# The value products of item s-1 move ahead of the first head's probability transposes of item s

## What is computed

```
q, k = rope(heads(h @ wq)), rope(heads(c @ wk));  v = heads(c @ wv)
a = softmax(q @ k^T / 8);  o = a @ v;  x = x + o @ wo + bo
```

## Time and profile before

| | us |
|---|---|
| median of 3 runs | 400.03 (399.65 to 401.43) |
| the profiled execution | 399.18 |
| its span, first to last instruction | 397.4 |
| outside the span (399.18 - 397.4) | 1.8 |
| PE busy | 377.9 (95%) |
| DVE busy | 304.4 (77%) |
| ACT busy | 294.5 (74%) |
| POOL busy | 171.1 (43%) |

### The profile page before, as it was taken

The page is one execution under the profiler, slowest core; times in us unless marked ns, Lnnn a source line. Parts: engine busy times, 40 slices in busy tenths (PEclk is TensorE's granted clock), DMA queues, the critical chain, the costliest instruction groups (busy, mean ns, idle before and its releaser), DMA issues.

```text
span 397.4 us, 9852 instructions
## 1 busy us (share of the span) xinstructions
PE 377.9 (95%) x3597; PEld 284.2 (72%) x3597; DVE 304.4 (77%) x655; ACT 294.5 (74%) x1023; POOL 171.1 (43%) x155
## 2 busy tenths in 40 slices
PE   7989999999999999999999898998999999999987
PEld 3557777776778777777777567775777778788665
DVE  4978998977888777988787758673658978888741
ACT  2377877877868778878787785779679787987932
POOL 4376544445555454554545334340365550302120
PEclk9999999999999999999999999999999999999999
DMA  7133333322333332332211200000000000000001
GB/s 231 54 123 120 107 126 107 120 101 103 125 115 107 106 106 87 129 123 84 81 68 67 82 27 28 2 2 1 2 2 2 2 3 2 2 3 2 2 0 53
DMA packets 17474, 25.90 MB, mean 65 GB/s; under 512 B 3631, under 2 KB 6194, under 8 KB 17426
## 3 DMA queue, kind: packets, MB, share of 16 engines
q1 hardware_dynamic: 17106, 25.05, 18.7%
q10 hardware_dynamic: 288, 0.22, 0.3%
q0 software_dynamic: 32, 0.00, 0.0%
HBM read 8.48 MB, written 0.52 MB: 23 GB/s over the span
## 4 chain that ended last, share of the span: by engine, by line
PE 61%; DVE 18%; ACT 10%; issue 6%; POOL 3%; DMA 1%; SPq 0%; DVEq 0%; POOLq 0%
PE bank L983 49%; PE bank L1069 7%; ACT prob L451 4%; PE bank L1279 4%; DVE nmax L859 3%; DVE xn L671 3%; ACT raw L537 2%; DVE prob L740 2%; DVE nmax L729 2%; DVE qk L771 2%; POOL xn L290 1%; DVE hT L682 1%; DVE qk L761 1%; DVE probT L754 1%; DVE st L656 1%
## 5 line engine op out<-in xcount | busy, mean ns | idle before, releaser
L309 POOL TENSOR_TENSOR swp<-swp,small 128x512 f32<-128x512 f32 x62 | 78.8, 1280 | 53.6 <-PE bank L983 31.7
L451 ACT ACTIVATE prob<-bank,nmax 128x128 f32<-128x128 f32 x256 | 91.5, 391 | 2.2 <-DVE nmax L729 2.2
L537 ACT ACTIVATE raw<-bank,nmax 128x128 f32<-128x128 f32 x256 | 72.9, 390 | 11.6 <-DVE nmax L859 11.3
L729 DVE TENSOR_REDUCE nmax<-bank 128x4 f32<-128x512 f32 x64 | 41.2, 686 | 33.0 <-PE bank L983 33.0
L451 ACT ACTIVATION_READ_ACCUMULATOR prob<-bank,nmax 128x1 f32 x256 | 59.3, 231 | 0.0
L355 POOL TENSOR_TENSOR prob<-prob,rz 128x512 f32<-128x512 f32 x29 | 30.2, 1042 | 58.0 <-DVE rz L734 58.0
L859 DVE TENSOR_REDUCE nmax<-bank 128x4 f32<-128x512 f32 x64 | 41.2, 685 | 17.1 <-PE bank L983 17.1
L983 PE MATMUL bank<-hT,wqkv 128*128 128x512 f32 x96 | 49.1, 595 | 0.2 <-DVE qk L761 0.2
L283 POOL TENSOR_TENSOR rstd<-vare,neg_half 128x4 f32<-128x4 f32 x12 | 12.3, 1024 | 84.1 <-DVE vare L663 84.0
L1069 PEld LDWEIGHTS bank<-small,prob 128*128 128x128 f32 x256 | 28.4, 140 | 24.3 <-DVE prob L740 13.4
L457 ACT ACTIVATE probT<-bank 128x512 f32<-128x512 f32 x32 | 19.1, 597 | 35.1 <-PE bank L1069 35.1
(11 more groups left out here) (114 smaller groups left out, 661.3 us busy)
## 6 DMA issues: line engine op xcount, KB each, us to landing
swp<-raw SPq DMA_DIRECT2D x124, 128.0 KB, 2.1
wqkv<-in_wqkv SPq DMA_DIRECT2D x16, 256.0 KB, 2.8
wff<-in_wff SPq DMA_DIRECT2D x4, 256.0 KB, 3.1
x<-in_x SPq DMA_DIRECT2D x2, 256.0 KB, 4.6
wmod<-in_wmod SPq DMA_DIRECT2D x2, 256.0 KB, 2.7
ctx<-in_ctx SPq DMA_DIRECT2D x1, 384.0 KB, 6.6
ctxT<-in_ctxT SPq DMA_DIRECT2D x1, 384.0 KB, 3.5
wsq<-in_wsq SPq DMA_DIRECT2D x1, 320.0 KB, 2.9
```

Source lines behind the costliest of these rows:

```text
L309: nc.gpsimd.tensor_tensor(four(swp[:, m % 2, f, :]), four(swp[:, m % 2, f, :]), sin[f], ALU.mult).then_inc(rope_sin[f], 1)
L451: last = nc.scalar.activation(prob[:, hh, bcols(u)], S[hh][:, bcols(u)], ACT.Exp, bias=nmax[:, s % 2, hh, u:u + 1], accum_out=zsum[:, s % ...
L537: last = nc.scalar.activation(prob1[:, s % 2, hh, bcols(u)], score_bank(s, hh)[:, bcols(u)], ACT.Exp, bias=nmax[:, s % 2, hh, u:u + 1])
L729: nc.vector.tensor_reduce(nmax[:, s % 2, hh, :], four(S[hh][:, :]), AX.X, ALU.max, negate=True).then_inc(rowmax[hh], 1)
```

## The change

In `l0_slot` of PE, for s = 1 to 29, the eight products `prob_values(s - 1)` are issued ahead of `transpose_probs(s, 0)` rather than behind it. Both keep their own waits. Nothing is added or removed, no transfer moves, and no other engine's list changes.

```diff
                 if s == 31:
                     prob_values(s - 1)
-                transpose_probs(s, 0)
                 if 1 <= s < 30:
                     prob_values(s - 1)
+                transpose_probs(s, 0)
                 if s == 28:
                     pe.wait_ge(exps[0], 29)
                     up(0, 0, 0, S[0])
```

## The result

The changed kernel takes 403.81 us (median of 8 runs) beside 400.11 for the kernel before (8 runs): ratio 1.0102, 95% interval 1.0081 to 1.0123, that is 4.1 us slower (3.2 to 4.9). Beside other runs later it was 1.0089 (1.0064 to 1.0115), 3.6 us. 402.9 had been forecast, 2.9 us slower. Its profiled execution took 404.01, with a span of 402.2.

A forecast was written before the change was run, and what follows sets the result against it. The prediction took PE's instruction list to bound the first layer. Terms 2.1 - 2.2 + 3.0 = +2.9 us took the median from 400.03 to 402.9; range for 8 in 10: 401.0 to 404.4.

The forecast's parts named there:

- What bounds the kernel: First layer is a race along PE's list; weight loads waited 13.4 us for DVE's division, but plain slots lose nothing to it.
- plain slots: Nine first-layer slots without background work or seed row, 6.64 to 6.65 us each, PE busy throughout.
- Part 1, the change of shape: Four array-shape changes per slot instead of three: +0.15 us in each of 14 slots where PE sets the pace, +2.1 us.
- The rival in which it is free: Shape changes cost nothing, covered by the wide fill or the queue: -0.8 us in all, 399.2; chance 0.09.
- The one in which waits at the head of PE's list hold the loads back: Value products' waits delay loads behind them by 0.05 to 0.1 us in 28 slots: 1.4 to 2.8 added, about 405; chance 0.08.
- Part 2, the stalls: Value products fill the transposes' wait for the division in slots 1, 4, 5, 7, 13, 21 and 28: -2.2 us.
- slots 4, 13, 21: Stall of 0.34 us less the 0.15 shape change: 0.19 gained in each, -0.57 us together.
- Slot 28: Transposes start 0.42 us late; number of shape changes stays the same, so the whole 0.42 is gained: -0.42 us.
- Slot 1: No output projection, short PE list; in the new order bound by the rope sum: -0.48 us, length 6.23.
- Slots 5 and 7: Stalls of 0.45 and 0.59 us, each less 0.15 for the shape change: -0.30 and -0.44 us.
- The sentence that no transfer moves and SP follows the slots: Side effects of the swap: no DMA moves, and SP and POOL follow the slots; no term in the sum.
- Part 3, the lost cover: Slots 6, 8, 9, 17, 25, 29: transposes no longer run while value products wait for bank O's readers; +3.0 us.

## Why the prediction was right, and by how much it was off

- **What bounds the kernel**: right. The load waits of 13.4 us were no loss in the plain slots; with them gone these slots are longer.
- **Part 1, the change of shape**: right to 0.01 us a slot (2.56 worked out, 2.57 seen; 0.15 in all 13 plain slots of three kernels). The rival in which it is free is out. The one in which waits at the head of PE's list hold the loads back is out for slots without a late copy; with one, three added waits right ahead of the transposes do cost 0.20, but in an arrangement that the changed kernel doesn't have.
- **Part 2, the stalls**: slots 4, 13, 21 gave 0.20 each (0.19 forecast), and with the old order slots 13 and 21 take 7.43 in every profile, so these stalls belong to the slots. Slot 28 gave 0.52, not 0.42: the wide products, which enter right after another shape, pay an entry of 0.10 that the sum had left out. Slot 1 is the step that failed. The sum gave it -0.48, read from one profile in which its copy was early. Where it is late the rope sum binds either order and the gain is 0; the two profiles of the changed kernel stand 0.45 and 0.75 above the profile that was read. Slots 5 and 7 failed in the same way, though their lengths came out (6.80 and 6.79 for 6.79 forecast). Their whole stalls of 0.45 and 0.59 were late copies: with early ones the old order takes 6.64 in both. In the changed kernel's first profile slot 5 had a copy nearly as late as before, and the order gave 0.13; in the second it was early and the order cost 0.15. In slot 7 the copy was early in both, so the order cost 0.15 there, and the 0.43 of difference is the copy's. That the forecast hit slot 7 is luck as far as the order goes. The sentence that no transfer moves and SP follows the slots missed why: slot 6, longer by 0.58, gives the copy of slot 7 that much more room.
- **Part 3, the lost cover**: 0.58, 0.59, 0.49, 0.40, 0.37 and 0.59 against 0.59, 0.59, 0.50, 0.40, 0.37 and 0.59. Missing was slot 15 in executions with a late copy, where the modulation read of bank O ends late, while the prediction took it to be over in time.
- **The total**: without slots 1 and 15 the sum was 2.9 + 0.48 - 0.15 = +3.2. Over slots 1 to 30, against the profile that was read, the changed kernel has 5.07 - 0.45 - 1.39 = +3.2 in its first profile and 4.13 - 0.75 - 0.15 = +3.2 in its second. That agreement rests on late copies in slots 5, 7 and 19 of the profile that was read. Against the second profile of the kernel before the same sums are 3.75 + 0.32 - 0.59 = +3.5 and 2.81 + 0.03 + 0.65 = +3.5: slot 5 then costs 0.15 instead of giving 0.29, slot 19 costs 0.15 instead of 0.02, and slot 7 gives 0.53. What was off was to take the copies of one execution as given. Had slot 1 been put at 0, the forecast would have been +3.4, 403.4. That lies within the intervals of both measurements, +3.6 (2.6 to 4.6) and +4.1 (3.2 to 4.9); lateness in slot 15 is a candidate for a share of what is left, and it was not separated from chance.

## What to carry to other kernels

A weight load's wait is not a stall: look whether the matmuls behind it still start at full pitch, and move work only in the places where they don't. Before two steps on one engine are swapped, ask of the later one whether it waits for something else: then the earlier one was its cover, and the swap pays it in full. Read a term that hangs on a transfer from several executions, since one may be lucky. And before a stall is booked as a gain, ask whether it belongs to the slot or to a transfer that came late that time: compare executions in which it came at the same moment.

## What the runs showed of the hardware

Switching PE between whole-array, column-tiled (value) and row-tiled (score) products cost 0.09 us on leaving a shape. Entering one cost 0.06 more (two transposes in 0.37 for 0.31) and 0.10 before wide products (the eight of `up` in slot 28: 229.97 - 226.34 = 3.63 in the kernel before, 234.23 - 230.70 = 3.53 in the changed one, where they follow transposes). A wide product ahead didn't hide the exit: 0.95 for 0.86 in slot 11.

The swapped copies, of equal size each time, let the second sine product end anywhere from 4.50 to 6.27 us into slot 1 from one execution to the next. Part of that spread is no transfer: in seven of the twelve profiles this product took 1.27 us and ended at 5.42 or earlier, in five it took 1.72 and ended at 5.98 or later. Between this product and DVE's division either can be the one that waits. In slot 1 of the changed kernel's first profile the division took 1.82 us and POOL's two products 2.51 together; in the second POOL began 0.11 later in the slot, the division took 0.70 and the two products 2.96 (start, duration, what; DVE and POOL of the first, then of the second):

```profile
27.61 1.82 DVE L740 TENSOR_TENSOR prob<-prob,rz 128x512 f32<-128x512 f32 x1
```

```profile
26.38 2.51 POOL L309 TENSOR_TENSOR swp<-swp,small 128x512 f32<-128x512 f32 x2 [1.76 <-DMA swp<-raw]
```

```profile
28.26 0.70 DVE L740 TENSOR_TENSOR prob<-prob,rz 128x512 f32<-128x512 f32 x1
```

```profile
27.14 2.96 POOL L309 TENSOR_TENSOR swp<-swp,small 128x512 f32<-128x512 f32 x2 [1.86 <-DMA swp<-raw]
```

In the first the division ended at 29.43, 0.54 after POOL's second product, somewhat less than its 0.70 alone, so most of it ran only then. The Trainium skill, "SBUF — State Buffer", Terms, describes a port pair that DVE and GpSimd take in turns, each for a whole instruction; these rows agree with it.
